# Dequantising 4-bit weights behind a transpose: turning packed bytes as 16-bit units and multiplying them by pre-split scales

## The reference

```python
low = W_packed & 15
high = W_packed >> 4 & 15
idx = jnp.stack([low, high], axis=-1).reshape(N, -1)      # two codes per int32 word, low one first
vals = NVFP4_LUT[idx]                                     # 0, 0.5, 1, 1.5, 2, 3, 4, 6 and their negatives
vals = vals.reshape(N, K // block, block) * scales[:, :, None]   # one fp32 scale per 32 values
...
gate = jnp.einsum('th,nh->tn', xt, Wg)
up = jnp.einsum('th,nh->tn', xt, Wu)
gelu = jnp.tanh(0.7978845608028654 * (gate + 0.044715 * gate ** 3)) * gate * 0.5 + gate * 0.5
out = jnp.einsum('tn,hn->th', gelu * up, Wd)
...
x = x + jnp.tanh(g_xattn[0]) * attention(layernorm(x), ...)
x = x + jnp.tanh(g_ffn[0]) * ffn(layernorm(x), ...)
```

## Time and profile before

| | |
|---|---|
| median of 3 runs | 334.01 us (332.62 to 334.28) |
| the profiled execution | 334.1 us, of which its span is 332.3 us |
| PE busy | 316.5 us, 95% of the span |
| DVE busy | 221.7 us, 67% |
| ACT busy | 157.8 us, 47% |
| POOL busy | 121.7 us, 37% |
| mean granted TensorE clock | 0.990 |

### The profile page before, as it was taken

One profiled execution on the slowest core, in us unless ns is written; L12 is line 12 of the kernel. 1 busy time (PEld: TensorE's weight loads), 2 busy tenths in 40 slices (PEclk: granted clock), 3 DMA queues, 4 the chain that ended last, 5 costly groups with the idle time before them and its releaser, 6 DMA issues.

```text
span 332.3 us, 4521 instructions
## 1 busy us (share of the span) xinstructions
PE 316.5 (95%) x1596; PEld 258.3 (78%) x1596; DVE 221.7 (67%) x458; ACT 157.8 (47%) x291; POOL 121.7 (37%) x118
## 2 busy tenths in 40 slices
PE   6977989999999999999999999999999999999996
PEld 5645778788767788788787887788778888888885
DVE  4786889997968458577585657658584544454545
ACT  2253746576545454355434454354355354434342
POOL 5333464566443223343232333233332233323331
PEclk9599999999999999999999999999999999999999
DMA  8950240000000000000000000000000000000001
GB/s 185 285 134 0 85 136 3 0 3 0 1 2 0 0 2 0 0 1 3 0 30 3 32 0 2 0 0 3 1 32 0 34 0 2 0 32 3 32 0 65
DMA packets 10838, 9.21 MB, mean 28 GB/s; under 512 B 3328, under 2 KB 8768, under 8 KB 10816
## 3 DMA queue, kind: packets, MB, share of 16 engines
q1 hardware_dynamic: 8144, 8.33, 8.6%
q10 hardware_dynamic: 2576, 0.59, 0.9%
q0 software_dynamic: 96, 0.01, 0.0%
HBM read 6.82 MB, written 2.10 MB: 27 GB/s over the span
## 4 chain that ended last, share of the span: by engine, by line
PE 74%; DVE 14%; ACT 5%; issue 3%; DMA 2%; POOL 1%; SPq 1%; DVEq 0%; ACTq 0%; POOLq 0%
PE ring_ps L1095 45%; PE acc_ps L1129 14%; PE acc_ps L1143 7%; DVE act L807 2%; DMA x_sb<-in_x_dram 2%; DVE act L813 2%; PE att_ps L1007 2%; DVE w_lo L786 1%; ACT act L549 1%; PE att_ps L1051 1%; ACT normed L528 1%; PE ring_ps L1087 1%; DVE w_lo L791 1%; PE att_ps L1059 1%; PE att_ps L1175 1%
## 5 line engine op out<-in xcount | busy, mean ns | idle before, releaser
L419 POOL TENSOR_TENSOR act_lo<-act,act_hi 128x512 fp32r<-128x512 f32 x63 | 81.7, 1297 | 153.3 <-ACT act_hi L560 153.3
L1095 PE MATMUL ring_ps<-xt_hi,w_hi 128*128 128x512 f32 (+1 forms) x262 | 105.7, 403 | 3.6 <-DVE w_lo L791 2.0
L1095 PE MATMUL ring_ps<-xt_lo,w_hi 128*128 128x512 f32 (+1 forms) x262 | 101.2, 386 | 0.0
L1095 PE MATMUL ring_ps<-xt_hi,w_lo 128*128 128x512 f32 (+1 forms) x262 | 101.0, 385 | 0.0
L549 ACT ACTIVATE act<-ring_ps 128x512 f32<-128x512 f32 x64 | 38.3, 598 | 106.3 <-PE ring_ps L1095 104.6
L807 DVE SCALAR_TENSOR_TENSOR act<-act,ring_ps 128x512 f32<-128x512 f32 x64 | 43.9, 686 | 60.3 <-ACT act L549 60.0
L813 DVE SCALAR_TENSOR_TENSOR act<-act,ring_ps 128x512 f32<-128x512 f32 x64 | 43.8, 685 | 26.9 <-ACT act L553 26.0
L1095 PEld LDWEIGHTS ring_ps<-xt_hi,w_hi 128*128 128x128 f32 x262 | 49.3, 188 | 15.3 <-issue 4.3
L1095 PEld LDWEIGHTS ring_ps<-xt_lo,w_hi 128*128 128x128 f32 x262 | 49.2, 188 | 10.5
L1095 PEld LDWEIGHTS ring_ps<-xt_hi,w_lo 128*128 128x128 f32 x262 | 49.4, 189 | 8.0
L553 ACT ACTIVATE act<-act 128x512 f32<-128x512 f32 x64 | 40.4, 633 | 22.0 <-DVE act L807 22.0
(11 more groups left out here) (110 smaller groups left out, 312.4 us busy)
## 6 DMA issues: line engine op xcount, KB each, us to landing
out_dram<-x_sb SPq DMA_DIRECT2D x8, 256.0 KB, 2.0
x_sb<-in_x_dram SPq DMA_DIRECT2D x1, 1024.0 KB, 7.6
packed<-L_ffn_gate_W_packed_dram SPq DMA_DIRECT2D x3, 256.0 KB, 2.9
packed<-n_L_ffn_up_W_packed_dram SPq DMA_DIRECT2D x3, 256.0 KB, 3.0
packed<-L_ffn_down_W_packed_dram SPq DMA_DIRECT2D x6, 128.0 KB, 4.0
ctx_sb<-in_ctx_dram SPq DMA_DIRECT2D x2, 384.0 KB, 7.8
x_sb<-in_x_dram SPq DMA_DIRECT2D x2, 256.0 KB, 4.4
x_sb<-in_x_dram SPq DMA_DIRECT2D x1, 512.0 KB, 6.3
```

The costliest lines, as they stand in the source:

```text
L419: pool.tensor_tensor(act_lo[:, s % RING, :], act[:, s % RING, :], act_hi[:, s % RING, :].bitcast(F32), ALU.subtract).then_inc(inter_lo, 1)
L1095: i = pe.matmul(into[:, tok], wt[:, n, w], xt[:, c % 2, k, tok], start=first, stop=(k, j) == last)
```

## The change

The scales no longer meet the codes before the transpose but after it.

- The DMA writes the packed words one byte off, so that the low byte of each word is the high byte of a 16-bit unit; two columns of zeros, cleared by POOL, stand between the blocks. PE turns these units as bf16, six transposes a pair (`turn_bytes`), into half a bank, and `compact` takes the bytes from PSUM.
- The scales are loaded as they are, turned once by PE (`turn_scales`), parted once into a bf16 high part (ACT) and an fp32 low part (DVE) (`split_scales`), and SP's DMAs copy the 8 rows that a unit needs to 16 partitions each, SBUF to SBUF (`spread_scales`, four DMAs a pair, two buffers).
- POOL multiplies codes by the high parts straight into `w_hi` and DVE codes by the low parts straight into `w_lo`, three instructions each a pair. ACT has no part in it, and `ring_ps` holds `gate` and `up` in a plain rotation.
- In the set-up the router is turned ahead of `x`, the second sequence's `x` is loaded and turned earlier, the layer norm of sequences 0 and 1 moves from DVE (`L743`) to ACT, `warm` matmuls are placed anew, and the second halves of four products (unit 1's `up` too) follow each other.

```diff
+        def turned_in(n):
+            return [n // 2 + 2] if n % 2 == 0 and 2 <= n and n // 2 + 2 < PAIRS else []
+        def rows_made_in(n):
+            return [(n + 3) // 2] if n % 2 == 1 and (n + 3) // 2 < PAIRS else []
+        def down_made_in(n):
+            return [n // 2 + 1] if n % 2 == 0 and 2 <= n and n // 2 + 1 < PAIRS else []
...
+            def spread_scales(r):
+                if r >= 2:
+                    sp.wait_ge(hi_made, 3 * (r - 1))
+                    sp.wait_ge(lo_made, 3 * (r - 1))
+                for v in range(2):
+                    u = 2 * r + v
+                    sp.dma_start(spread[:, r % 2, v * ROW_W:(v + 1) * ROW_W],
+                                 scales_rows[u * NB:(u + 1) * NB, :].unsqueeze(1).to_broadcast([NB, P // NB, ROW_W])
+                                 ).then_inc(rows_spread[r], 16)
+                for a in range(KT):
+                    row, at = (a * PAIRS + r) * NB, 2 * ROW_W + a * DOWN_W
+                    sp.dma_start(spread[:, r % 2, at:at + DOWN_W],
+                                 scales_down[row:row + NB, :].unsqueeze(1).to_broadcast([NB, P // NB, DOWN_W])
+                                 ).then_inc(down_spread[r], 16)
...
             load_x(0, 1, x_loaded[0])
+            load_x(1, 2, x_loaded[1])
+            sp.wait_ge(packed_cleared, 2)
...
+            sp.wait_ge(scales_split, 2)
+            spread_scales(0)
+            for m in range(2):
+                load_rows(2, m)
+            load_down(2)
+            spread_scales(1)
...
-                pool.tensor_tensor(w_nat[:, r % 2, i * GU:(i + 1) * GU].rearrange("p (b k) -> p b k", k=BLK // 2),
-                                   codes, s, ALU.mult).then_inc(scaled, 1)
+            def rows_high(u):
+                pool.wait_ge(unpacked, u // 2 + 1)
+                pool.wait_ge(rows_spread[u // 2], 16 * 2)
+                pool.tensor_tensor(rows_place(u, 0), rows_codes(u), rows_scales(u, 0), ALU.mult).then_inc(hi_made, 1)
...
-            def rows_high(u):
-                sc.wait_ge(tile_turned, tile_of(u) + 1)
-                sc.activation(w_hi[:, u, 0:GU], bank_of("tile", tile_of(u)), ACT.Copy,
-                              scale=FP4_SHIFT).then_inc(rows_hi, 1)
...
             def rows_low(u):
-                dve.wait_ge(rows_hi, u + 1)
-                dve.scalar_tensor_tensor(w_lo[:, u, 0:GU], bank_of("tile", tile_of(u)), FP4_SHIFT,
-                                         w_hi[:, u, 0:GU].bitcast(F32), ALU.mult, ALU.subtract).then_inc(rows_lo, 1)
+                dve.wait_ge(unpacked, u // 2 + 1)
+                dve.wait_ge(rows_spread[u // 2], 16 * 2)
+                dve.tensor_tensor(rows_place(u, 1), rows_codes(u), rows_scales(u, 1), ALU.mult).then_inc(lo_made, 1)
...
+            def turn_bytes(r):
...
+                elif r > 2:
+                    pe.wait_ge(inter_done, 2 * r - 4)
+                words = packed[:, r // 2 % 2, r % 2, :]
+                for o in range(SEGS):
+                    v, m = divmod(o, 2)
+                    at = WORDS[m] + v * P if o < 4 else WORDS[2 + m]
+                    units = words[:, at:at + P].bitcast(BF16).rearrange("p (j two) -> p j two", two=2)[:, :, 0]
+                    i = pe.transpose(bytes_bank(r)[:, o * P:(o + 1) * P], units, ident_b[:, :])
+                i.then_inc(bytes_turned, 1)
...
             def gate(s):
                 c, n = divmod(s, UNITS)
                 if c == 0:
-                    pe.wait_ge(rows_lo, n + 1)
+                    pe.wait_ge(hi_made, parts_of(n))
+                    pe.wait_ge(lo_made, parts_of(n))
...
-                bank_free("gate", s)
+                pe.wait_ge(gated, s - 1)
```

More of the change, by code:

```diff
@@ L303, in normed_bank, with down_place @@
+        def down_place(r, part):
+            return (w_hi, w_lo)[part][:, 2 * r:2 * r + 2, GU:CODES].rearrange("p i (a n) -> p i a n", a=KT)
         def normed_bank(b):
@@ L442, in _ @@
                     s = c * UNITS + n
[L443 to L445 removed]
                     if s >= 1:
                         low_part(s - 1)
+                    if c == 0:
+                        for r in rows_made_in(n):
+                            for u in (2 * r, 2 * r + 1):
+                                rows_high(u)
                     for b in next_sequences(c, n, STATS_1):
```

440 lines of the change are left out of this document (190 added, 250 removed).

## The result

The changed kernel takes 353.7 us (median of 4 runs, 352.1 to 354.9) against 334.1: ratio 1.0595 [1.0535, 1.0654]. It is 19.7 us slower, where 329 was forecast. Its profiled execution took 352.1 us, of which 350.5 are its span.

The account below looks back on a forecast made before the run. PE and DVE were both taken as near full where weights are made, with DVE becoming the bound of steps 3 to 12. Sum: 334.1 - 2.5 - 1.8 - 0.3 - 0.7 = 328.8, said as 329; range 325.2 to 335.8.

Parts of the forecast that it names:

- Spreading the scales: 0 if it is in time.: SBUF-to-SBUF copies of scales: no cost if in time, 590 KB a pair needing 2 to 5 us.
- the spreading is late: Rival: copies reading only 8 partitions move at 40 GB/s, 14.9 us a pair; slower, 344; chance 0.12.
- the 11 us a pair: Copy time of a pair's scales by the skill page's 27 GB/s a port, two of 16 ports reached.
- Set-up, 2.5 us less.: Start to gate(2): second sequence's statistics and xt_lo(1) come earlier; gate(2) at 33.2 from 35.75, 2.5 us less.
- `gate(2)` to `gate(3)`, 1.8 less.: Early stretch of 7.93 us: two waits and two tiles go, six bf16 transposes (0.53) come in; 1.8 us less.
- Steps 3 to 12, 0.3 less.: Stretch of 53.62 us making weights beside steps: PE loses 15 tiles, but DVE's waits for POOL leave 53.3, 0.3 less.
- the forecast 0.37: Mean wait in us of each of DVE's 15 low parts for POOL in steps 3 to 12, resting on list order.
- I leave 2.0. So 53.3, DVE the bound: Steps 3 to 12: DVE works 51.3 us plus 2.0 idle, making 53.3; DVE is the bound and PE has waits.
- Steps 13 to 15, 0.7 less.: Stretch of 15.16 us: DVE has 6 us free, so two tiles off PE count fully; 0.7 us less.
- The rule on the lock: Skill page: a two-SBUF-input DVE instruction and a GpSimd instruction reading SBUF exclude each other throughout; each new low part can wait.
- 344 for whole multiplies: Total in us if each of the 15 new low parts met a whole POOL multiply, instead of 329.
- the 338 of its rival: Rival that POOL costs more than taken: at a mean wait of 1.06 us, slower, 338; chance 0.05 for slower.

Follow-up runs that it names:

- f_loads_first: Changed kernel with the loads of pair 2's packed words, x and context ahead of the wait for the parted scales in SP's list: 347.3 us.
- n_spread_fixed: Changed kernel, reference's output: loads ahead of the spreading, scale columns reordered by ACT so source partitions lie 4 apart: 344.3 us.
- a_all_ports: Changed kernel with each spreading DMA reading its source from all 128 partitions instead of 8 (wrong scales): 345.1 us.
- m_low_on_pool: n_spread_fixed with down's low part on POOL, weigh ahead of DVE's second rows_low, and rows_high(2), (3) ahead of down_high(0) on POOL: 340.0 us.
- s_shift: m_low_on_pool with shift moved from DVE to POOL behind the root, DVE writing the negated mean for it: 336.2 us.
- v_weave: s_shift with a new attention table, giving sequences 2 and 3 later steps for some stages; reference's output: 333.5 us.
- k_pool_memset: a_all_ports with POOL's 24 high parts filled with a constant, reading nothing; not the reference's output: 335.9 us.
- p_neither: a_all_ports with both DVE low parts using a constant instead of scales and POOL high parts as memsets; not the reference's output: 333.5 us.
- g_one_input: a_all_ports with DVE's 24 low parts multiplying codes by a constant, one SBUF input instead of two; not the reference's output: 336.3 us.
- w_neither_weave: p_neither with a new attention table, giving sequences 2 and 3 later steps for some stages; not the reference's output: 329.4 us.
- t_before_sbuf: Kernel before the change with DVE's 24 low parts reading w_hi twice, both inputs in SBUF; not the reference's output: 335.4 us.

## Why the prediction was wrong, point by point

The account, in medians, goes best by the kernels that compute the reference's output. From 353.7, SP's order takes 6.4 us off (f_loads_first), other source partitions 3.0 more (n_spread_fixed, 344.3); a_all_ports, with the order left, gets 8.6 by the source alone, so the two don't add up. Then `down_low` on POOL and `weigh` earlier take 4.3 (m_low_on_pool, 340.0), `shift` on POOL 3.7 (s_shift, 336.2), and room in the attention's table 2.7 (v_weave, 333.5). That is the whole loss, and none of the forecast gain. The kernels with another output show what is left: from a_all_ports at 345.1, a shorter low part takes 8.8 off, memsets on POOL 9.3, both 11.6, and the table 4.1 more, to 329.4.

*"Spreading the scales: 0 if it is in time."* This step failed first: a term put at nothing that cost 9.4 us. It priced the copies at 2 to 5 us a pair by the rate of DMAs from HBM and by "half as many engines at today's rate". Measured: 10.5 us a pair, 56 GB/s in the mean. The rival "the spreading is late" named the mechanism and its point of decision, 9 us a pair; it took 14.9 and came out at 344. It missed that SP is held 3.3 us by an issue behind a slow copy, so that loads in the same queue are late too: 6.4 us by f_loads_first. Of the prediction's figures the 11 us a pair beside that rival came closest. It also put the loss into all pairs, and it lay nearly all in the set-up and the first steps; from pair 3 on no engine waited for `spread`.

*Set-up, 2.5 us less.* Came out 5.5 more, through the spreading and, in a_all_ports, still 0.7 more (`gate(2)` at 36.4). With POOL's multiplies gone it is at 33.6 (k_pool_memset) and 33.5 (p_neither), while another form of the low part alone leaves it at 36.3 (g_one_input). So with memsets on POOL the list comes out near the 33.2 forecast, and the term missed that the multiplies hold DVE's other instructions there: `shift` takes 1.04 us twice and `probs` 1.07 in a_all_ports.

*`gate(2)` to `gate(3)`, 1.8 less.* 5.65 us in a_all_ports and 6.55 in the changed kernel, for 6.1: right in kind. The six bf16 transposes cost 0.32 us (45.22 to 45.54 in the changed kernel), not 0.53.

*Steps 3 to 12, 0.3 less.* 67.96 for 53.3; 65.3 with fast copies. The mean wait of a low part was right: 1.18 - 0.69 = 0.49 for those of rows and 0.04 for those of down, over 12 and 6 (`down_low` takes 726 ns) a mean of 0.34 us for the forecast 0.37. Unpacking lost 1.6 us of its excess in a_all_ports, not 3.0, and `probs` (1.23 us each for 0.29 before) and `shift` (1.2 for 0.15) were held in place of `lead`. The step that failed is "I leave 2.0. So 53.3, DVE the bound": in a_all_ports DVE works 56.9 us (2.1 of them because eleven instead of ten steps of `act` fall into the stretch) and is idle 8.4, of which 5.5 for ACT's `square` and `tanh`, and PE works 51.1 of 65.3. Neither engine is full. What sets the time, as I read the waits, is a chain that goes PE, ACT, DVE, ACT, DVE and back in every step, and twice through the attention; an instruction held inside that chain costs its wait on DVE, then a stop of PE, and then the slow clock (0.95 over the stretch, for 1.00 before). s_shift shows it for one kind of instruction, 2.1 us of waits for 3.7 of time; for the stretch as a whole it is argued. DVE being the bound was my reading of 48.8 busy of 53.6; it was really a sum of work, which is not the same as a path.

*The table.* No term had it. Taking 5.7 us of work off PE makes a step shorter, and whatever spans a fixed number of steps then has less time. Before, PE reached `probs` and `normed` without a wait; in p_neither it waits 5.6 us for the attention. This is where most of the expected gain went in p_neither: the new table gives 4.1 us back there.

*Steps 13 to 15, 0.7 less.* 0.6 less. *The last 220 us* are unchanged (220.1), and packed loads one byte off land as before where the copies are fast (256 KB after 3.0 us in a_all_ports, 2.9 before).

*The rule on the lock.* The prediction's 344 for whole multiplies is a slip of its sum: by its own terms DVE would have 48.8 + 15.9 - 3.0 + 2.0 = 63.7 us, 10.1 over the stretch, and the total 339, beside the 338 of its rival.

*What the agreement with 329 is worth.* For p_neither and w_neither_weave a reservation stands: their low part takes 0.42 us where nothing holds it, not 0.68, so 24 x 0.26 = 6 us of DVE's work is missing, and their agreement with 329 is in part that. Also, a kernel with the whole work done and the blocking gone wasn't made: v_weave, the best one with the reference's output, still has `w_lo` of rows held beside POOL (1192 ns in the median), and it is level with the kernel before. In the old order of the lists only 3 of the 16 were held (1.17, 1.00 and 1.17 us in t_before_sbuf, with two of the eight parts of down at 0.9); whether a new order can have that too wasn't tried and stays open.
